# Cross-attention kernel: the scores' shift moved from VectorE to GpSimd, the guard folded, the small split placed later

## What is computed

```python
xn = layernorm(ctx, ln_x_g, ln_x_b)              # (8, 1601, 192)
ln = layernorm(_layernorm(x), ln_l_g, ln_l_b)    # (8, 64, 256)
q = ln @ Wq.T
kv = concatenate([xn @ Wkv.T, ln @ Wlkv.T], axis=1)
qn = q / max(sqrt(mean(q * q)), 1e-8) * qn_g * DH ** -0.5     # per head
kn = k / max(sqrt(mean(k * k)), 1e-8) * kn_g
attn = softmax(where(mask, qn @ kn.T, -big))
x = x + (attn @ v) @ Wo.T + bo
```

## Time and profile before

| | us |
|---|---|
| median of 3 runs | 520.67 (520.42 to 523.8) |
| profiled execution | 520.81, its span 519.0 |
| busy PE / DVE / ACT / POOL over the span | 431.1 / 405.3 / 237.8 / 250.3 |
| TensorE's mean granted clock | 0.964 |

### The profile page before, as it was taken

The page is one execution under the profiler, slowest core; times in us unless marked ns, Lnnn a source line. Parts: engine busy times, 40 slices in busy tenths (PEclk is TensorE's granted clock), DMA queues, the critical chain, the costliest instruction groups (busy, mean ns, idle before and its releaser), DMA issues.

```text
span 519.0 us, 6624 instructions
## 1 busy us (share of the span) xinstructions
PE 431.1 (83%) x2042; PEld 334.5 (64%) x2042; DVE 405.3 (78%) x969; ACT 237.8 (46%) x547; POOL 250.3 (48%) x264
## 2 busy tenths in 40 slices
PE   3786557779799889887998988887997877899996
PEld 0364335567677677675786867774474765678885
DVE  5847799999999999999988896625659556887776
ACT  0238645267466564664654744331233125335551
POOL 5451956658558557576484553001431232445550
PEclk9999988889999999999899999899999988889999
DMA  8605842022141041222200000920000000000001
GB/s 248 179 1 148 237 135 56 2 90 53 51 141 50 3 141 50 76 67 58 90 3 1 1 1 15 406 97 0 0 2 0 1 0 0 1 1 1 0 2 41
DMA packets 23976, 31.80 MB, mean 61 GB/s; under 512 B 2955, under 2 KB 19653, under 8 KB 23941
## 3 DMA queue, kind: packets, MB, share of 16 engines
q1 hardware_dynamic: 23940, 31.38, 19.6%
HBM read 30.69 MB, written 0.52 MB: 60 GB/s over the span
## 4 chain that ended last, share of the span: by engine, by line
DVE 34%; PE 30%; POOL 21%; issue 8%; ACT 4%; DMA 2%; SPq 1%; DVEq 0%; POOLq 0%; ACTq 0%
PE bank L573 29%; POOL kr L483 12%; DVE kss L1397 5%; DVE arena L1409 4%; DVE arena L1445 3%; DVE split_b L1388 3%; POOL crs L448 3%; DVE cst L1334 2%; DVE arena L1604 2%; DVE arena L1618 1%; DVE kguard L1400 1%; POOL split_b L472 1%; DVE big L1319 1%; POOL cguard L449 1%; DMA mask_in<-in_p_mask 1%
## 5 line engine op out<-in xcount | busy, mean ns | idle before, releaser
L573 PE MATMUL bank<-keyq,split_b 128*128 128x512 f32 (+2 forms) x724 | 171.0, 384 | 21.2 <-DVE split_b L1678 6.7
L573 PEld LDWEIGHTS bank<-keyq,split_b 128*128 128x128 f32 (+1 forms) x724 | 124.7, 194 | 51.3 <-issue 18.0
L483 POOL TENSOR_TENSOR kr<-kguard,neg_half 128x8 f32<-128x8 f32 (+1 forms) x56 | 94.4, 1686 | 103.5 <-DVE kguard L1400 103.1
L573 PE MATMUL bank<-arena 128*128 128x193 f32 (+4 forms) x528 | 103.4, 340 | 18.5 <-ACT arena L1133 9.0
L573 PEld LDWEIGHTS bank<-arena 128*128 128x128 f32 (+2 forms) x528 | 86.9, 195 | 31.1 <-issue 13.9
L1126 ACT ACTIVATE arena<-bank 128x512 f32<-128x512 f32 (+1 forms) x56 | 31.5, 563 | 59.9 <-PE bank L573 59.4
L573 PE MATMUL bank<-split_b,keyq 128*128 128x512 f32 x204 | 51.7, 405 | 0.1
L1409 DVE TENSOR_TENSOR arena<-bank,kr 128x512 f32<-128x512 f32 (+1 forms) x56 | 36.1, 645 | 19.3 <-POOL kr L483 19.1
L1388 DVE TENSOR_TENSOR split_b<-arena,split_b 32x256 fp32r<-32x256 f32 (+1 forms) x112 | 48.0, 428 | 2.5
L573 PEld LDWEIGHTS bank<-split_b,keyq 128*128 128x128 f32 x204 | 39.1, 197 | 8.0 <-DVE split_b L1669 0.2
L472 POOL TENSOR_TENSOR split_b<-arena,split_b 128x256 fp32r<-128x256 f32 (+1 forms) x56 | 38.2, 682 | 10.1 <-ACT split_b L1109 10.0
(11 more groups left out here) (222 smaller groups left out, 620.5 us busy)
## 6 DMA issues: line engine op xcount, KB each, us to landing
arena<-in_ctx SPq DMA_DIRECT2D x16, 576.0 KB, 4.4
arena<-in_p_ctxT SPq DMA_DIRECT2D x8, 800.5 KB, 6.7
arena<-in_p_ctxT SPq DMA_DIRECT2D x8, 400.2 KB, 7.1
arena<-in_p_experts SPq DMA_DIRECT2D x1, 2688.0 KB, 18.4
arena<-in_p_experts SPq DMA_DIRECT2D x1, 2304.0 KB, 12.2
arena<-in_p_experts SPq DMA_DIRECT2D x1, 1536.0 KB, 6.4
X<-in_x SPq DMA_DIRECT2D x1, 512.0 KB, 3.7
arena<-in_t_Wlkv SPq DMA_DIRECT2D x1, 512.0 KB, 7.0
```

What stands on the lines that cost most here:

```text
L483: pool.tensor_tensor(kr[0:r, n % 2, 0:k], kg_[0:r, n % 2, 0:k], neg_half[0:r, 0:4 * k].rearrange("p (t h) -> p t h", h=H), ALU.pow).then_i ...
L573: return nc.tensor.matmul(out_, l, r, start=start, stop=stop, skip_group_check=shared)
```

## The change

Four edits, all in the cross-attention.

1. `shift_scores` runs on GpSimd. At `g` 2 and 3 it stands behind the power of the step, else between the split's rest and the power. GpSimd's loop now runs over all `steps`.
2. `cguard` and its instruction on GpSimd (L449, 16 of them) are gone. The clamp takes `cve` with the factor 64e-16 and the maximum with the plain sum of squares. The missing factor 1/64 inside the power is made good by leaving 64 ** -0.5 out of `qkg`, and the latent scores get it in their copy.
3. `split_high` holds the 128 channels alone; the rest is `split_small`, with a semaphore of its own (`xs_small`), and it alone waits for the deviations. It follows at once, but at `g == 5` (the first group of the next batch) it comes behind the exponentials and the squares.
4. GpSimd waits for the split of the channels alone, VectorE's `split_side` for the small one.

```diff
@@ GpSimd
-                then(pool.tensor_scalar(cguard[:, k, of], cve[:, k, of], 1e-16, None, ALU.mult))
...
+            def shift_scores(m):
+                b, g = divmod(m, NG)
+                if g == 0:
+                    pool.wait_ge(mbc_evac, b + 1)
+                v = sn[b % 2]
+                if g < NG - 1:
+                    pool.tensor_tensor(v[:, 2 * g:2 * g + 2, :], v[:, 2 * g:2 * g + 2, :], mbc[:].unsqueeze(1).broadcast_to([P, 2, D]), ALU.subtract).then_inc(shifted, 1)
+                else:
+                    then(pool.tensor_tensor(v[0:TAIL, FULL, :], v[0:TAIL, FULL, :], mbc[0:TAIL, :], ALU.subtract))
+                    pool.tensor_tensor(lat_tile(b), lat_tile(b), mbc[lat_rows(b), :], ALU.subtract).then_inc(shifted, 1)
+                    pool.wait_ge(shifted, m + 1)
...
-            for u in range(groups):
+            for u in range(steps):
...
+                if g not in (2, 3) and 0 <= u - SHIFT < groups:
+                    shift_scores(u - SHIFT)
...
-                key_scales(u)
+                if u < groups:
+                    key_scales(u)
+                if g in (2, 3) and 0 <= u - SHIFT < groups:
+                    shift_scores(u - SHIFT)
@@ ScalarE
-                    act.wait_ge(sd_in[b % 2], 32 * (b // 2 + 1))
...
+            def split_small(n):
+
+                b, g = divmod(n, NG)
+                if g == 0:
+                    act.wait_ge(sd_in[b % 2], 32 * (b // 2 + 1))
...
+                A(xs[n % 3][0:96, 2:4, 0:k], ctxT[b % 2][0:96, 1:2, 256 * g:256 * g + k].broadcast_to([96, 2, k]), ACT.Copy).then_inc(xs_small, 1)
...
+                    if g != 5:
+                        split_small(u + 2)
...
+                if g == 5 and u + 2 < groups:
+                    split_small(u + 2)
@@ VectorE
-                dve.wait_ge(xs_split, n + 1)
+                dve.wait_ge(xs_small, n + 1)
...
-                V.scalar_tensor_tensor(kg_[0:r, n % 2, 0:k], kss[0:r, n % 2, 0:k], 1.0 / DH,
-                                       cguard[0:r, b % 2, 2 * g:2 * g + k].unsqueeze(2).broadcast_to([r, k, H]), ALU.mult, ALU.max).then_inc(k_ss, 1)
+                V.scalar_tensor_tensor(kg_[0:r, n % 2, 0:k], cve[0:r, b % 2, 2 * g:2 * g + k].unsqueeze(2).broadcast_to([r, k, H]), DH * 1e-16,
+                                       kss[0:r, n % 2, 0:k], ALU.mult, ALU.max).then_inc(k_ss, 1)
```

More of the change, by code:

```diff
@@ L1107, in split_high @@
                 k = 256 if g < NG - 1 else TAIL
-                A(xs[n % 3][:, 0, 0:k], ctxT[b % 2][:, 0, 256 * g:256 * g + k], ACT.Copy)
-                A(xs[n % 3][0:96, 2:4, 0:k], ctxT[b % 2][0:96, 1:2, 256 * g:256 * g + k].broadcast_to([96, 2, k]), ACT.Copy).then_inc(xs_split, 1)
+                A(xs[n % 3][:, 0, 0:k], ctxT[b % 2][:, 0, 256 * g:256 * g + k], ACT.Copy).then_inc(xs_split, 1)
+            def split_small(n):
+                b, g = divmod(n, NG)
+                if g == 0:
+                    act.wait_ge(sd_in[b % 2], 32 * (b // 2 + 1))
+                k = 256 if g < NG - 1 else TAIL
+                A(xs[n % 3][0:96, 2:4, 0:k], ctxT[b % 2][0:96, 1:2, 256 * g:256 * g + k].broadcast_to([96, 2, k]), ACT.Copy).then_inc(xs_small, 1)
             def scale_context(n):
@@ L1148, in evac_latent_scores @@
                     act.wait_ge(y_mm, b - 3)
[L1149 removed]
+                A(lat_tile(b), spare_bank(b)[lat_rows(b), 0:D], ACT.Copy, scale=DH ** -0.5).then_inc(ls_evac, 1)
             def evac_turned_sum(b):
@@ L1180, in _ @@
             evac_queries()
-            split_high(0)
-            split_high(1)
+            for n in range(2):
+                split_high(n)
+                split_small(n)
             for j in range(4):
@@ L1496, in _ @@
             last.then_inc(wkv_scaled, 1)
-            V.scalar_tensor_tensor(qkg[:], qg[:], DH ** -0.5, kg[:], ALU.mult, ALU.mult).then_inc(qkg_ready, 1)
+            V.tensor_tensor(qkg[:], qg[:], kg[:], ALU.mult).then_inc(qkg_ready, 1)
             norm_apply(0, X, xn)
@@ L1537, in _ @@
                     norm_apply(2, X, big)
-                if g not in (2, 3) and 0 <= u - SHIFT < groups:
-                    shift_scores(u - SHIFT)
                 if u < groups:
@@ L1547, in _ @@
                     max_diagonal(b - 1)
-                if g in (2, 3) and 0 <= u - SHIFT < groups:
-                    shift_scores(u - SHIFT)
                 if u + 2 < groups:
```

14 lines of the change are left out of this document (1 added, 13 removed).

## The result

| | kernel before | changed kernel |
|---|---|---|
| median (runs in the same comparison) | 522.0 us (520.4 to 523.8) | 528.9 us (527.9 to 531.4) |
| ratio to before | 1 | 1.014, interval 1.008 to 1.020 |
| profiled execution, its span | 520.8, 519.0 | 529.9, 528.1 |
| first power of the loop at | 52.7 | 54.6 |
| from the first power to the last (56 groups), "the loop" | 269.3 | 276.0 |

The last four lines are read from the starts of the power in the trace. The forecast was 527.0, so the time is 1.9 us above it. Of the 9.1 us between the two profiled executions the loop has 6.6. The late first power has 1.9: TensorE's granted clock is 0.91, 0.84 and 0.91 in the three stretches of 10 us from 30 to 60, where the kernel before has 1.00, and its products of the setup take longer.

The account below looks back on a forecast made before the run. A cycle through VectorE and GpSimd was taken to bound the kernel. 520.8 plus 7.5 for the shifts less 1.4 for guards in batches 0 and 1 gave 526.9, said as 527; range 515 to 534, the main case's own 523 to 531.

Parts of the forecast that it names:

- the 50 that was named as the limit: GpSimd's wait for VectorE's clamp over the whole execution should fall from 103 to under 50 us.
- The walk through the batch: Cross-attention loop, the batch of 188.30 followed group by group: a batch becomes about 1.1 us longer.
- "late" values: How much later each group's power starts than before: 1.0, 0.4, 0.45, 0.1, 0.6, 1.1 us for groups 1 to 6.
- The one step left open, group 4: Two shifts run on GpSimd here and either engine may get in first; taken as late by 0.1 us (-0.2 to +0.4).
- The guard: Batches 0 and 1 lose four more guards on GpSimd's path, without shifts to pay for: -1.4 us.
- Rival (d): Guard's fold and deferral do all and the shift is neutral: 519 us; counted with Rival (a).
- I take nothing; it could give back 0.3 a batch, or cost 0.6: Deferred deviations: the spread starts up to 3.5 us later and lands about when the small split is reached; counted as nothing.
- Rival (c): The late spread or later shifts reach ScalarE and TensorE: another 1 us a batch, 534 us; chance 0.12.
- Rival (a): VectorE's maximum gets in ahead of GpSimd's shift; a batch ends about 0.4 us shorter, 517 us; chance 0.15.
- the power starts at T+2.7: With VectorE first, the next power starts 2.7 us after the last power's end T, instead of T+2.93; groups 5 and 6 gain 0.2 each.
- Rival (b): The engines do not hold each other in a way that matters: 2.6 us less a batch, 502 us; chance 0.18.
- The rule on the port pair: A two-SBUF-input VectorE operation starting just behind a two-input GpSimd one waits until that ends; the power does not hold VectorE.

Follow-up runs that it names:

- Run 8: Changed kernel with GpSimd's 128x512 shift replaced by a same-size one-operand operation that leaves out subtracting the maximum: 514.8 us, 0.986 of the kernel before.
- run 4: Changed kernel in which the shift, where it stands ahead of the power, also waits for VectorE's maximum of the group before: 525.4 us, 1.006 of the kernel before.
- run 7: Kernel before with only the guard folded into the clamp: 518.6 us, 0.993 of the kernel before.
- run 1: Changed kernel with the shift back on VectorE at its old places, guard's fold and deferral kept: 520.8 us, 0.996 of the kernel before.
- run 6: Changed kernel without the deferral, the deviations waited for at the first split again: 538.2 us, 1.031 of the kernel before.

## Why the prediction was right

**The mechanism held, step by step.** The shift took 1284 ns (forecast 1.30). It began 0.69 after the split's rest. The maximum asked 0.11 behind it (forecast 0.08) and ended 0.55 after its end (0.55). Its mean in batches 2 to 6 is 1.53 (forecast about 1.5; 1.35 over the whole execution), the batch of 192.01 is 36.26 (36.2). GpSimd's wait for the clamp is 53.3, a little above the 50 that was named as the limit. Run 8 shows that this is a matter of the two operands, and run 4, in which the maximum keeps 0.69 and the loop is 6.1 us shorter, that it costs the loop's time.

**The walk through the batch.** Mean growth of each step in batches 2 to 6, against the differences of the "late" values:

| step from group | 0 | 1 | 2 | 3 | 4 | 5 | 6 | sum |
|---|---|---|---|---|---|---|---|---|
| forecast | +1.0 | -0.6 | +0.05 | -0.35 | +0.5 | +0.5 | 0 | +1.1 |
| measured | +0.74 | -0.48 | +0.09 | -0.09 | +0.45 | +0.46 | +0.07 | +1.24 |

The one step left open, group 4, went to GpSimd, by 0.10 us:

```profile
210.69 1.31 POOL L483 TENSOR_TENSOR arena<-arena,side 128x512 f32<-128x512 f32 x1
210.79 1.76 DVE L1450 TENSOR_TENSOR arena<-arena 128x512 f32<-128x512 f32 x1
```

That is 0.26 a batch. The step from group 0 came out 0.26 shorter than forecast, so that the good sum of a batch is in part luck. The loop grew by 6.6 us against 6.1 forecast. The other 2.5 us by which the profiled execution (529.9) is above the forecast of 526.9 are the first power's 1.9 and 0.5 behind the loop.

**The guard.** Its fold was counted at 1.4 in batches 0 and 1, which is what run 7 shows there (1.3). In the later batches it was inside the walk, as part of groups 1 and 2, where it is 0.85 a batch by itself. Guard and deferral without the shift are run 1: 520.8, and by its ratio 1.6 us less than the kernel before (guard alone, run 7: 3.4 less). Rival (d) had 519, 1.8 less than before, for a change whose shift is neutral; its size is about right, but the shift is not neutral.

**The deferral was right only in its sum.** The step "I take nothing; it could give back 0.3 a batch, or cost 0.6" saw that the spread would come later, and that the small split would meet it. It did not price what the later spread would have done without the deferral: 10 us of loop (run 6 against the changed kernel). A delay and its cover stood in one change and cancelled. Rival (c), TensorE waiting more often for the exponentials, stayed out (5.5 us against 9.0 before).

**Rival (a) was priced wrong, and would not have been faster.** Its step "the power starts at T+2.7" forgot that the clamp has two operands in SBUF as well. Run 4 makes the case by hand: 525.4, not 517, and a loop of 269.9 in place of the 265 that the forecast of (a) comes to. Rival (b) needed the maximum to keep 0.7; run 8, in which it nearly does, is at 514.8 and not 502, since steps 0 and 1 are as long as in the changed kernel, with GpSimd at work almost without a break from the end of one power to the next; what bounds the rest was not tried.

**The rule on the port pair.** The rule of the Trainium skill (SBUF — State Buffer, "SBUF: two separate sides"), that the loser stands for the winner's whole instruction, agrees with the trace for the shift: the maximum ended 0.55 us behind its end. It does not for run 8's one-operand operation, which reads SBUF too: the maximum ended 0.34 us ahead of its end. Of the power the prediction said that it does not hold VectorE. That is so for 128 rows (the pair keeps 0.85 inside 1.86), but not for the 65 rows of a batch's last group: there the pair took 1.28 in the kernel before already, and ended with the power.

## What to carry to other kernels

Before work goes from VectorE to GpSimd, look at what VectorE does at that moment: an operation with two operands in SBUF that begins just behind a two-operand one on GpSimd costs VectorE the whole of it, and even a clamp of 8 values a partition does. Put such work under VectorE operations that read PSUM or have one operand, step by step and only where GpSimd has slack; here three of seven so placed were 2.5% faster than all seven in the queue's order. Compare with moving nothing too: the guard's fold with every shift left on VectorE had a loop of 263.8 us, with three shifts moved it was 266.1, with four 263.4 and in the best order 261.2, so that the move itself is hardly shown to pay. Measure parts of a change in both directions, since a deferral that is worth nothing alone was worth 9 us beside the shift. And before a few microseconds are put down to an edit, look where in the execution they lie and what TensorE's clock was there.
